# The split weights of v of the next layer, loaded right behind those of q and k

## What is computed

```python
# DIM = 128, HEADS = 16, DIM_HEAD = 64, INNER = 1024, WINDOW = 32, DEPTH = 6
def attn_layer(x, Wqkv, qs, ksc, Wo):
    qkv = x @ Wqkv                               # Wqkv[i] is 128 x 3072
    q, k, v = jnp.split(qkv, 3, -1)
    q, k, v = (sh(q), sh(k), sh(v))              # 16 heads of 64
    q = l2norm(q) * qs
    k = l2norm(k) * ksc
    q = q * cos * scale + rotate_half(q) * sin * scale
    k = k * cos * inv + rotate_half(k) * sin * inv
    out = local_attention(q, k, v)               # windows of 32, each sees itself and the one before
    return out @ Wo

for i in range(DEPTH):
    x = attn_layer(shift_tokens(x), Wqkv[i], q_scale[i], k_scale[i], Wo[i]) + x
    x = ffn_layer(shift_tokens(x), ln_g[i], ln_b[i], W1[i], b1[i], W2[i], b2[i]) + x
```

## Time and profile before

| | |
|---|---|
| time, median of 3 runs | 4168.06 us (4167.7 to 4170.24) |
| the profiled execution | 4166.94 us, of which the span is 4165.0 |
| PE busy | 3739.9 us, 90% of the span |
| DVE, POOL, ACT busy | 79%, 66%, 59% |
| mean granted clock of TensorE | 0.977 |
| the stack | from about 729 us to the end |

### The profile page before, as it was taken

The page is one execution under the profiler, slowest core; times in us unless marked ns, Lnnn a source line. Parts: engine busy times, 40 slices in busy tenths (PEclk is TensorE's granted clock), DMA queues, the critical chain, the costliest instruction groups (busy, mean ns, idle before and its releaser), DMA issues. The chain is left out here.

```text
span 4165.0 us, 109635 instructions
## 1 busy us (share of the span) xinstructions
PE 3739.9 (90%) x42284; PEld 2929.0 (70%) x42284; DVE 3285.1 (79%) x4472; ACT 2478.0 (59%) x3301; POOL 2737.2 (66%) x2200
## 2 busy tenths in 40 slices
PE   5998895899998999989999989999899998999996
PEld 3766673677776777767777777777677777777774
DVE  4666664788888888878888878888788888888884
ACT  2555553566666666656666656666566665666663
POOL 2454541777776777766777766767677776677772
PEclk9999997999999999999999999999999999999998
DMA  1121211222223222232222222222322223222222
GB/s 41 56 86 63 73 48 51 59 67 52 68 53 96 63 59 58 59 93 62 65 55 62 81 67 64 58 59 60 87 73 51 66 53 91 63 64 58 59 59 61
DMA packets 157178, 267.01 MB, mean 64 GB/s; under 512 B 32062, under 2 KB 51644, under 8 KB 152380
## 3 DMA queue, kind: packets, MB, share of 16 engines
q1 hardware_dynamic: 157116, 266.19, 23.8%
HBM read 44.81 MB, written 26.21 MB: 17 GB/s over the span
## 5 line engine op out<-in xcount | busy, mean ns | idle before, releaser
L817 POOL TENSOR_TENSOR st_qk_rot<-st_qk_rot,st_qk_sq 128x1024 f32<-128x1024 f32 x384 | 920.2, 2401 | 864.3 <-DVE st_qk_sq L714 864.3
L457 PE MATMUL st_ps<-st_wqkv,st_xs 128*128 128x512 f32 x3456 | 958.6, 413 | 105.4 <-issue 36.7
L457 PEld LDWEIGHTS st_ps<-st_wqkv,st_xs 128*128 128x128 f32 x3456 | 613.4, 191 | 277.0 <-issue 133.6
L837 POOL TENSOR_TENSOR st_qk_rot<-st_qk_rot,st_rn 128x1024 f32<-128x1024 f32 x384 | 723.5, 1905 | 15.1
L565 ACT ACTIVATE st_qk_sq<-st_ps 128x1024 f32<-128x1024 f32 x384 | 393.8, 1025 | 541.0 <-PE st_ps L457 540.4
L696 DVE TENSOR_REDUCE st_nt<-st_qk_sq 128x16 f32<-128x1024 f32 x384 | 465.6, 1212 | 253.6 <-ACT st_qk_sq L565 253.3
L714 DVE TENSOR_TENSOR st_qk_sq<-st_ps,st_rot 128x512 f32<-128x512 f32 x768 | 490.2, 678 | 0.0
L700 DVE TENSOR_TENSOR st_qk_rot<-st_ps,st_rot 128x1024 f32<-128x1024 f32 x384 | 465.8, 1213 | 8.4 <-PE st_ps L472 8.4
L472 PE MATMUL st_ps<-consts_sb,st_qk_rot 128*128 128x128 f32 x3072 | 402.4, 274 | 29.5 <-DVE st_hid L797 16.8
L472 PEld LDWEIGHTS st_ps<-consts_sb,st_qk_rot 128*128 128x128 f32 x3072 | 356.1, 141 | 95.7 <-DVE st_hid L797 36.6
L465 PEld LDWEIGHTS st_ps<-st_oT,st_wo 128*128 128x128 f32 x3072 | 369.0, 192 | 68.3 <-issue 67.6
(11 more groups left out here) (141 smaller groups left out, 6640.5 us busy)
## 6 DMA issues: line engine op xcount, KB each, us to landing
st_v_bd<-st_v_tok SPq DMA_DIRECT2D x1152, 128.0 KB, 2.4
st_v_bd<-st_v_tok SPq DMA_DIRECT2D x672, 64.0 KB, 2.1
wqkv_parts<-at_w_parts SPq DMA_DIRECT2D x18, 1024.0 KB, 4.6
st_wqkv<-wqkv_parts SPq DMA_DIRECT2D x18, 1024.0 KB, 5.6
at_w_raw<-in_wqkv SPq DMA_DIRECT2D x18, 512.0 KB, 5.1
rotary_tables<-at_rot SPq DMA_DIRECT2D x6, 512.0 KB, 3.4
st_rot<-rotary_tables SPq DMA_DIRECT2D x24, 128.0 KB, 2.4
st_wo<-in_wo SPq DMA_DIRECT2D x6, 512.0 KB, 4.5
```

Of the source, the lines that this page charges most:

```text
L457: last = pe.matmul(out[:, c * 512:(c + 1) * 512], xs[:, x_part, t * P:(t + 1) * P], rhs, start=(n == 0), stop=(n == len(PASSES) - 1))
L817: pool.tensor_tensor(qk_rot[:, cols], qk_rot[:, cols], qk_sq[:, cols], ALU.add).then_inc(rot_done[a], 1)
L837: pool.tensor_tensor(view, view, rn[:, par, heads_of(a)].unsqueeze(2).to_broadcast([P, HEADS, DH]), ALU.mult).then_inc(normed[a], 1)
```

## The change

In a layer's last unit, before the spreading of tile 3, SP now also waits for v's matmuls of that tile and issues the load of v's weights behind those of q and k. The load after the last tile's spreading and table is gone. The bytes, the number of DMAs and everything on the other engines are the same; SP has one wait more in each of the five passages from one layer to the next.

```diff
                         if what == "wqkv" and t == TILES - 1:
 
-                            for kind in "qk":
+                            for kind in "qkv":
                                 sp.wait_ge(ready[kind], tiles_done(u, 0, t))
                                 load_wqkv(layer + 1, kind)
                         spread_v(u, t)
...
                             load_table(layer + 1, t)
-                    if what == "wqkv":
-
-                        load_wqkv(layer + 1, "v")
```

## The result

The changed kernel takes 4109.31 us in the median of four runs (4108.14 to 4116.39), the kernel before, run beside it, 4167.88. The ratio is 0.9864, 95% interval 0.985 to 0.9879: 1.4% faster, 58.6 us. The forecast was 4110, with a range of 4106 to 4118.

The account below looks back on a forecast made before the run. PE was taken as the bound, standing still for v's weights at five passages. Removing 57.5 us (35.3 wait, 6.3 v's slow matmuls, 15.9 later effects) from 4166.9 gives 4109.4, or 4110.6 by the median; forecast 4110, range 4106 to 4118.

Parts of the forecast that it names:

- The sum: Over the five layer passages, all 57.5 us lost against the steady pace go, giving 4110 us.
- The other 22 us: Passage loss beyond PE's 35.3 us wait: 6.3 v's slow matmuls, 15.9 slow transposes and the later wait with slow clock.
- The cause named for the larger part: Before L522, VectorE's L771 takes 2.15 us instead of 0.50, blocked on shared ports by GpSimd's L837, begun 0.03 us earlier.
- The landing: At the passage, v's load issued about 1817.5 lands at 1827.3, 1.4 us before PE wants it; no residual wait.
- k's row plus a megabyte: Basis for v's landing: k's at 1824.8 plus 2.5 us for one more megabyte, so 1827.3.
- the bound: Upper bound on v's landing: longest of 18 loads, 10.6 us, so 1828.1, 0.6 us before PE wants it.
- An issue that gets stuck: On SP, v's issue might stick behind megabytes in flight; nearest row 4.86 us, ending at 1822.4, at zero cost.
- the cover that was named: On SP, 5.9 us between v's issue ending at 1817.9 and the spreading's first issue at 1823.85.
- The carried rows: First two spreading pieces of tile 3 land at 1827.3 to 1828.1, not about 1826; 3 us margin for ScalarE, cost zero.
- first rival: At the passages v lands 0.6 to 2 us late, each microsecond costing 5: 4113 to 4120; chance 0.10.
- third rival: At the passages q, k, v loads share engines evenly, landing together; q 3.2 us late: 4125 to 4148; chance 0.03.

## Why the prediction was right

**The sum.** Right to 0.1 us in the trace: 57.5 us forecast, 57.6 gone from the 45 distances. It was taken from the distance of one instruction once a unit, against the pace of an undisturbed one, not from the line of waits, which showed 35.3. Who had taken the waits alone would have forecast 4132.

**The other 22 us.** Said to be consequences of the standstill. The runs show it: without a wait in the passage the surplus is nothing, and with waits of 35.3, 29.4, 16.3 and 6.7 us in all it is 22.2, 21.4, 20.3 and 19.6 (with q last 16.4 and 16.1, behind 1.44 MB 13.0 and 15.4). So it does not grow in proportion to the wait. But that the first four are so near each other is a coincidence, for their parts differ. PE's order of time, the five passing units against a steady one, in us:

| | before | spreading held back |
|---|---|---|
| longer wait at L522 (L524) | 6.9 | 8.7 |
| its slow matmuls | 7.1 | 5.5 |
| v's slow matmuls | 6.3 | 0 |
| wait before the next tile's q | 0 | 7.4 |
| the rest | 1.9 | -2.0 |

The cause named for the larger part, L771 behind L837, holds in a stronger form than it was argued: taking the step off VectorE leaves 5.9, and where the same kernel has both orders of the two instructions, the surplus goes with the order.

The Trainium skill's rule on the shared pair of ports ("SBUF — State Buffer", section "SBUF: two separate sides") fits in kind: 2.15 us when GpSimd begins 0.03 us ahead, with a multiply of 1.90 us, and 0.50 when it begins later. Blocked for the whole multiply the step would have taken 1.87 + 0.50 = 2.37, 0.22 us more than it did. The section limits the rule to VectorE instructions in a two-port mode or with two inputs in SBUF; no run here shows whether L771 is in such a mode, while L672, late in the run with the spreading held back, has two such inputs. That GpSimd catches up during the standstill, and is therefore 1 us earlier against VectorE, is read from the order of time and not tested by itself.

**The landing.** v was issued 1.1 us after q (forecast 1.0), and its landing, 10.1 us, lies between k's row plus a megabyte (9.8) and the bound (10.6). Margin forecast 1.4, at least 0.6; measured 1.0 at this passage, but 0.5 in the other profiled execution, where v took 10.6 us, the bound itself, and was issued 0.1 later than forecast. The bound rests on one load of one trace; that it held is in part luck, for a landing half a microsecond longer would have brought a wait. An issue that gets stuck was provided for, and one did, for 1.1 us, under the cover that was named. The Trainium skill's figure of 358 GB/s ("DMA: Bandwidth & Descriptors", section "Specifications") would have left 0.3. The trace does not bear it out: the stretches of one microsecond from 1813 to 1820 in the profile after show 377 to 442 GB/s.

**The carried rows.** Expected 1.3 to 2.1 us later behind v's data. They land after 2.9 and 3.8 us instead of 2.0 each, the second 1.8 later, and nobody waits.

**What was wrong, though the result does not show it,** is the price of the first rival, "each microsecond costs 5, so 4113 to 4120". A v that lands a little late costs the phase as well: with 1.3 us in each passage the kernel takes 4135, with 2.6 us 4138. Had the margin been used up, the time would have lain outside the range. The weak step is the one that priced a short standstill by its length, though the rows of before showed that 22 us of 57 did not come from its length. The third rival's sharing of the engines is refuted for loads ahead; for transfers behind a load something of it is true (4.9 against 6.9 us).

## What to carry to other kernels

Measure a stall by the distance between two marks of the work, against an undisturbed round, and not by its line in the list of waits: here more than a third of the cost stood elsewhere, and it was about as large for a standstill of 1.3 us as for one of 7, though made of other parts. Where a transfer is needed at a fixed point and its queue has slack earlier, issue it as soon as its place is free, and count the landing with all that is queued ahead of it and soon behind it. When an instruction at times takes four times its length, look which engine began a moment before it; moving that one instruction to an engine with room brought 38 us with the wait left as it was, and shortening the wait from 7 to 3.3 us brought 21.

## What the runs showed of the hardware that was not expected

- Transfers issued behind a load slow it down: 1 MB lands 4.8 to 5.1 us after its issue with nothing behind it (in the kernel before, with ten DMAs and a table ahead of it, and with the spreading held back), and 6.5 to 7.2 with four or eight DMAs of 128 KB issued right behind. Behind two other megabytes, with the spreading 6 us behind, it lands after 8.8 to 10.6 us.
- A pause of PE that was 0.27 us longer (1.93 instead of 1.66, once a unit) went with a granted clock that fell in 26 of 46 units, at a cost of 1.7 us each; at 1.66 it fell in no steady unit. Whether the 0.27 us or the other order of work is what tips it was not tested. The length of the pause alone does not decide: with the spreading held back it was 3.37 to 3.40 us in all five passing units, and the same twelve matmuls took 7.11, 5.41, 8.13, 6.83 and 5.41 us.
- A DMA issue on SP that takes 0.34 us took 1.44 and 1.45 as the third megabyte in a row, at the second passage in both profiles of the changed kernel, and at none of their other eight passages; with v first and q last it did so at none of five.
